# Taking ten products of constants out of each routed slot of attention, in a fused embedding, attention and expert kernel

## What is computed

```python
h = concat([layernorm(patches @ W.T + b) * gamma + beta, vocab[x_txt]], axis=1)     # 32 x 68 x 192
# attention on x = layernorm(h): 12 heads of 16; each query keeps 32 keys
q, k, v = split(x @ qkv_w.T + qkv_b)
pred = einsum("bhnd,bhmd->bhnm", ex_quant(q), ex_quant(k))     # powers of two; chooses the keys
idx = top_k(pred, 32)
attn = softmax over idx of (q . k / 4)
h = h + (attn @ v) @ proj_w.T + proj_b
# experts on x = layernorm(h)
w_fk, w_rk = top4(softmax((x @ W_fk + b_fk) @ norm(emb_fk).T)), ...      # 128 experts each
h = h + restore(feature(x, f_know, w_fk), r_know, w_rk)
```

## Time and profile before

| | |
|---|---|
| median of 3 runs | 949.04 us (945.45, 949.04, 955.71) |
| the profiled execution | 945.62 us |
| its span, first to last instruction | 943.9 us |
| PE busy | 789.4 us (84%) |
| DVE busy | 653.0 us (69%) |
| POOL busy | 564.5 us (60%) |
| ACT busy | 362.7 us (38%) |
| mean clock granted to TensorE | 0.842 of full speed |

### The profile page before, as it was taken

The page is one execution under the profiler, slowest core; times in us unless marked ns, Lnnn a source line. Parts: engine busy times, 40 slices in busy tenths (PEclk is TensorE's granted clock), DMA queues, the critical chain, the costliest instruction groups (busy, mean ns, idle before and its releaser), DMA issues.

```text
span 943.9 us, 22303 instructions
## 1 busy us (share of the span) xinstructions
PE 789.4 (84%) x6357; PEld 659.8 (70%) x6357; DVE 653.0 (69%) x4126; ACT 362.7 (38%) x1147; POOL 564.5 (60%) x788
## 2 busy tenths in 40 slices
PE   5789999999999889888874699999988799399800
PEld 3678888888888678777653477999866458356700
DVE  2198899899999799888867577666753354155433
ACT  0123444444444354535322333444422357345700
POOL 5255676676766567575468517406776677775075
PEclk9788899999999588778655599999997899799955
DMA  9322543544514233634019498756899798499533
GB/s 326 116 95 107 190 165 138 187 146 157 185 64 165 89 116 98 188 103 133 16 50 283 151 288 276 211 146 184 255 405 408 249 335 286 147 300 369 192 100 92
DMA packets 81696, 177.25 MB, mean 188 GB/s; under 512 B 12968, under 2 KB 38344, under 8 KB 78760
## 3 DMA queue, kind: packets, MB, share of 16 engines
q1 hardware_dynamic: 56200, 120.62, 38.2%
q10 hardware_dynamic: 14112, 32.12, 9.1%
q0 software_dynamic: 11264, 23.09, 8.1%
HBM read 94.25 MB, written 81.53 MB: 186 GB/s over the span
## 4 chain that ended last, share of the span: by engine, by line
PE 45%; POOL 25%; issue 11%; ACT 8%; DMA 6%; DVE 4%; SPq 1%; POOLq 0%; ACTq 0%; DVEq 0%
PE bank L1056 6%; POOL early L782 6%; PE bank L1036 5%; PE bank L1356 5%; PE bank L1304 5%; PE bank L1292 4%; PE bank L1358 3%; PE bank L1309 3%; POOL qbd L646 3%; POOL eqbd L655 3%; PE bank L1104 3%; PE bank L1346 3%; PE bank L1081 3%; POOL slots_g L789 3%; POOL slots_x L758 2%
## 5 line engine op out<-in xcount | busy, mean ns | idle before, releaser
L1441 DVE MATCH_REPLACE8 work<-top,work 128x68 f32<-128x68 f32 x896 | 179.5, 213 | 0.0
L1435 DVE MAX8 top<-work 128x8 f32<-128x68 f32 x896 | 129.7, 215 | 32.6 <-ACT tru L832 29.2
L1747 DVE COPY place<-bank 96x256 f32<-96x256 f32 x147 | 56.9, 416 | 64.3 <-PE bank L1292 62.4
L782 POOL DMA_INDIRECT early<-slots_h,s_all x68 | 65.7, 966 | 57.7 <-DMA slots_h<-m_y 37.6
L1036 PE MATMUL bank<-early,xp 128*128 128x192 f32 x432 | 92.3, 378 | 7.0 <-DMA xp<-in_a_x 5.1
L758 POOL DMA_INDIRECT slots_x<-early,s_all x68 | 68.0, 1001 | 46.8 <-DVE s_all L1633 27.2
L1036 PEld LDWEIGHTS bank<-early,xp 128*128 128x128 f32 x432 | 89.4, 231 | 9.0 <-DMA xp<-in_a_x 5.4
L782 POOL DMA_INDIRECT early<-slots_y,s_all x68 | 65.0, 955 | 50.9 <-DMA slots_y<-m_y 29.0
L1755 DVE COPY place<-bank 128x128 f32<-128x128 f32 x147 | 37.5, 287 | 81.4 <-PE bank L1346 81.1
L706 POOL TENSOR_TENSOR sc<-work,tru 128x476 f32<-128x476 f32 x32 | 38.0, 1189 | 83.3 <-ACT work L886 83.3
L789 POOL DMA_INDIRECT slots_g<-early,s_all x68 | 66.3, 976 | 27.4 <-issue 20.1
(11 more groups left out here) (202 smaller groups left out, 1896.0 us busy)
## 6 DMA issues: line engine op xcount, KB each, us to landing
early<-slots_x SPq DMA_DIRECT2D x49, 384.0 KB, 3.8
slots_y<-m_y ACTq DMA_DIRECT2D x49, 384.0 KB
slots_h<-m_y ACTq DMA_DIRECT2D x49, 256.0 KB
early<-slots_g SPq DMA_DIRECT2D x49, 256.0 KB
f_all<-in_f_know SPq DMA_DIRECT2D x16, 768.0 KB, 9.6
r_all<-in_r_know SPq DMA_DIRECT2D x16, 768.0 KB
slots_x<-zero SPq DMA_DIRECT2D x28, 360.0 KB, 3.0
slots_x<-zero SPq DMA_DIRECT2D x28, 336.0 KB, 3.3
```

What stands on the lines that cost most here:

```text
L782: nc.gpsimd.indirect_dma_start(g_in[:, i % DEPTH, k, 0:width], None, src, bass.IndirectOffsetOnAxis(s_all[:, r - 1, i, k:k + 1], 0)).then_ ...
L1435: last = nc.vector.max(top8[:, c, :], work[:, par, c, :])
L1441: last = nc.vector.match_replace(work[:, par, c, :], top8[:, c, :], work[:, par, c, :], TAKEN)
L1747: nc.vector.tensor_copy(m_xT[t][0:HALF], turn_bank[t][0:HALF, 0:2 * P].rearrange("p (c s) -> p c s", c=2)).then_inc(sem["m_xt0"], 1)
```

## The change

`keep_busy` is taken out. The wait for `t_placed`, which stood ahead of the ten products, stays in its place, now directly ahead of `t_position(i - 1)`. All other instructions, on all engines, are the same and in the same order; line numbers of what follows fall by eight, or by seven after the call.

```diff
-            def keep_busy(i):
-
-                if i >= 2:
-                    pe.wait_ge(sem["t_placed"], i - 1)
-                for n in range(10):
-                    nc.tensor.matmul(ps_spare[:, 2 * NE:4 * NE], ones_b[:], zero[:, 0:128].bitcast(BF16), start=False, stop=False,
-                                     skip_group_check=True)
-
             def slot(b, m):
@@
                 if i is not None:
                     t_logits(i)
-                    keep_busy(i)
+                    if i >= 2:
+                        pe.wait_ge(sem["t_placed"], i - 1)
                     if i >= 1:
                         t_position(i - 1)
```

## The result

The changed kernel takes 968.54 us (median of four; 963.93 to 971.42), the kernel before 947.44 us over its four runs beside it. The ratio of the two, new over old, is 1.023, with a 95% interval of 1.0193 to 1.0268: slower by 2.3%. The forecast was 963 us and slower by over 1%.

A forecast was written before the change was run, and what follows sets the result against it. PE was taken to bound half-clock slots, POOL and ACT full-clock ones. Staying at half clock, +18.9 us, less 4 for one rise, gave +15: 960.6 from the profiled execution, 964.0 from the median; 963 us chosen, range 947 to 971.

The forecast's parts named there:

- The bound: Routed slots: PE sets the pace at half clock (16.97 us), POOL and ACT with the attended output at full clock (14.10).
- The clock: Routed slots: the ten products raise TensorE's clock; without them it stays at 0.50 from 308 us on.
- The sum for a slot: PE's list at half clock, start to start, is 17.58 us; over slots 22 to 30 this adds 18.9 us.
- the edit's own gain: 90 products removed at unchanged clock: nothing per full-clock slot, 0.38 us per long slot, 1.5 us in all, at most 8.6.
- slot 30 with its end: Last changed slot: loses 2.14 us of products, pays them back in scores at half clock, so 0.
- B: Routed slots: clock still rises every second slot, on values, logits and scores; about +4 us, 953 us; chance 0.18.
- C: Routed slots: clock doesn't depend on the ten products; -1.5 us, at most -8.6, 947 us likely; chance 0.09.
- D: Expert products behind the slots: half-clock phases shift, some us either way, possibly 970 us or more in total; chance 0.05.
- Rises that still happen: Values to first scores, 2.8 us nearly as dense as the ten, may raise the clock; one rise taken, 4 us off.
- The Trainium skill's rule: Whole kernel: ramp penalty under 1% of a typical span, so at most 9.4 us; not taken for the sum.

The follow-up runs named there:

- even slots only: Kernel before, with the ten products kept only in slots 22, 24, 26, 28 and 30: 948.64 us, ratio 0.9998.
- twenty products: Kernel before, with twenty products instead of ten behind the logits in slots 22 to 30: 952.49 us, ratio 1.0056.
- thin products: Kernel before, each routed slot's ten dense products replaced by five fp32 products of 16 columns with identity weights: 986.89 us, ratio 1.0425.
- the spread ones without attend's four: Variant with products at both places and around attend, minus the four in the middle of attend: 943.68 us, ratio 0.996 to the kernel before.
- the spread kernel: Variant with ten behind logits and ten ahead of the tile's turn, plus four behind the turn and four mid-attend: 938.77 us, ratio 0.9906.

## Why the prediction was right

**The bound.** Right in the main. PE was said to be what a half-clock slot waits for and POOL and ACT, with the attended output between them, what a full-clock slot waits for. The changed kernel has PE busy 17.50 of 17.50 us; even slots only and twenty products show that PE's load behind the logits makes no difference to a slot at full clock. The chain that ends last in the kernel before's slot from 398.73 on runs, with other pieces between, through

```profile
398.73 1.59 PE bank L1056 x16
401.35 1.70 POOL qbd L646 x2
412.60 0.18 ACT xnT L816
```

that is POOL from 401.35 to 409.55 and ACT from there on. PE's queries-and-keys product opens it, and the attended output is not in it.

**The clock.** Right, and shown: thin products of the same length leave it low, five raise it in most slots and not in all, ten in slot 22 alone raise it there and into slot 23.

**The sum for a slot.** 17.58 predicted, 17.50 measured, term by term from slot 26 of the changed kernel against the prediction's:

| | predicted | measured |
|---|---|---|
| queries and keys | 2.63 | 2.52 |
| tile's query, attend, values, logits | 0.95, 2.68, 1.32, 0.85 | 0.95, 2.68, 1.32, 0.85 |
| positions and turned output | 0.65 | 0.66 |
| scores | 4.54 | 4.53 |
| projection, turned probabilities and norm | 1.34, 0.97, 0.25, 0.97 | 1.34, 0.97, 0.26, 0.97 |
| turn of the tile | 0.43 | 0.45 |

Slot 26 before had a wait of 0.32 us ahead of the queries-and-keys product, which the closed-up list has not; that the 0.11 us too much in the first term comes from it is likely, but was not tried. By slots: 17.16 and 17.37 predicted for 22 and 23, 17.18 and 17.28 measured; up to slot 30's start +18.9 predicted and 139.46 - 121.07 = +18.4 measured; slot 30 with its end +0.2 where 0 was put.

**What hid the edit's own gain.** In a slot at full clock nothing, shown by the run with even slots only, as predicted. The 0.38 us for a long slot whose clock stayed as it was could not be measured by itself, because no kernel has such a slot without the products; twenty products show the other side of it, ACT's wait growing by about half a microsecond and the slot by about 0.5 to 1.1.

**The rivals.** B (rises in every second slot) and C (a clock that does not need the ten) fell with the clock row of after; D, a loss in the stages behind, would have been in the third part of the execution, which became 1.3 us shorter. That holds for the profiled execution; a loss of D's kind is real, for three experiments have it in theirs (below), and whether the slower runs of the changed kernel have it too is open.

**Rises that still happen: wrong.** One rise was put in, -4 us. From 308.9 us to 479.6 there was none in the profiled execution. The step that failed is that values, logits, positions, turned output and the first scores "may do" for a rise. No run before had shown it, and it did not come once in nine slots. With it left out the sum would have been 945.6 + 18.9 = 964.5 for the lower execution (963.93 measured) and 967.9 for the median (968.54). Rival B, which gave the range its room down to 947 us, rests on the same premise, that this work is nearly as dense as the ten. The 4 us for a rise that did not come, and 963 us chosen below the median's own sum of 964, are why the forecast lies 5.5 us under the measured median. That it is so close is also a matter of which runs the median fell on: the four differ by 7.5 us.

**The Trainium skill's rule.** The prediction read "the ramp penalty is <1% of a typical kernel span" (the Trainium skill, TensorE: Matmul & The Clock Gate, section on the clock gate) as a bound of 9.4 us on the change, and did not use it for the sum. The change cost 2.3%, 21.1 us by the medians. The sentence is on the ramp of a typical kernel; here the clock had fallen and risen again all through the routed slots, and without the ten products it stayed at 0.50 for 171 us on end.

**Left open.** Medians differ by 21.1 us, the two profiled executions by 18.3. Both profiled ones are at the lower end of their runs. A part of what the runs of one kernel spread by can be seen in the traces. From slot 31's attend to the end, ten of the thirteen profiled executions take 481.27 to 483.20 us, and in these the clock rises 1.5 to 2.2 us after the first expert product begins. Ten products in slot 22 alone take 488.25 there, the thin ones 490.69 and the spread ones without attend's four 494.51, and in these three the rise comes 14 to 20 us after that start, though nothing in this part was changed. What decides this was not tried. It means that a difference of up to some 12 us between two medians can come from behind the slots; the longer half of the runs with ten products ahead of the turn, 12 us above the others, may be such a case, but they were not profiled.

## What to carry to other kernels

Before work that "does nothing" is taken out of PE, look at the granted clock on both sides of it and at what PE did before each rise; if the rise follows the idle products, price the step by the half-clock durations of the whole slot, not by their own 2 us. When such products are to hold the clock, count where PE is thin and spread them over those places, idle time first: ten in one place bought about every second slot, 28 in four places seven in a row, and 24 in three of these places six of seven. Thin products with the same busy time only did harm here. And before a difference of some us between two variants is put down to the edit, cut both traces into the same stages: here one variant lost nothing in the slots that were edited and 11.6 us in a stage that was not.

## What the runs showed of the hardware

- A busy share of 1.00 on PE says nothing of the clock that it will get: PE was 19.44 of 19.44 us busy at 0.50 with thin products, and 10.17 of 14.10 at 1.00 with even slots only.
- PE that is busy without a hole can stay at half clock for long and then get full clock in the same work: 20.10 of 20.10 us at 0.50 in the first expert product of one execution, where the same products had a mean of 0.95 over the same length in another.
- The ten products multiply zeros with ones, and the clock rises behind them all the same: each of its rises in slots 22 to 30, in all kernels with such products, comes 0.8 to 4.2 us after the start of a set of them.
- The products of attend, 68 rows by 17 columns in fp32, move only 17 columns but load 68 columns of weights, and they too go at nearly half speed at half clock: 24 records in 2.68 us at 0.50 and 12 in 0.71 us at 1.00 (384.41 to 385.12 in the spread kernel).
- Small steps can be on two sides of the path by clock: four products in attend cost nothing in slots at full clock (14.1 us with and without), while slots that start low took 16.84 to 18.07 us with them and 16.43 to 16.97 without.
